# Attention walk of a decoder layer: written out without loops, with rotated queries and later tokens' inputs turned by DMA instead of by TensorE

## What is computed

```
q = rmsnorm(x @ w_qa, q_norm_w) @ w_qb                  # 16 heads of 128 + 64
q_nope, q_rope = (q[..., :DN], q[..., DN:])
kv = x @ w_kva
kv_c, k_rope = (kv[..., :KV_LORA], kv[..., KV_LORA:])
kv = rmsnorm(kv_c, kv_norm_w) @ w_kvb
...
q_rope = q_rope * cos + rotate_half(q_rope) * sin
k_rope = k_rope * cos + rotate_half(k_rope) * sin
scores = einsum('blhd,bmhd->bhlm', q, k) * scale        # causal mask
attn = softmax(scores)
out = einsum('bhlm,bmhd->blhd', attn, v).reshape(B, L, H * DV) @ w_o
```

## Time and profile before

| | |
|---|---|
| median of 3 runs | 1381.97 us (1381.57 to 1382.5) |
| profiled execution | 1380.98 us, its span 1379.2 us |
| PE busy | 1052.4 us, 76% |
| DVE busy | 1100.2 us, 80% |
| ACT busy | 539.6 us, 39% |
| POOL busy | 237.3 us, 17% |
| DMA, queue that SP issues to | 85.12 MB, 25.2% of 16 engines |
| granted TensorE clock, mean | 0.911 |
| DMA transposes | 256, median landing 2.8 us |

### The profile page before, as it was taken

One profiled execution on the slowest core, in us unless ns is written; L12 is line 12 of the kernel. 1 busy time (PEld: TensorE's weight loads), 2 busy tenths in 40 slices (PEclk: granted clock), 3 DMA queues, 4 the chain that ended last, 5 costly groups with the idle time before them and its releaser, 6 DMA issues.

```text
span 1379.2 us, 27210 instructions
## 1 busy us (share of the span) xinstructions
PE 1052.4 (76%) x7460; PEld 634.8 (46%) x7460; DVE 1100.2 (80%) x2984; ACT 539.6 (39%) x1225; POOL 237.3 (17%) x475
## 2 busy tenths in 40 slices
PE   1635587898988989989989999999652643447998
PEld 0423354555555555555555555555241322224554
DVE  5679587888888887987988888888169788886886
ACT  1549434443333434334333434344023330534443
POOL 1000012121121112112112112111003323122111
PEclk9659899999999999999999999999875766778999
DMA  9100022332322242222342232344560110000001
GB/s 361 47 1 0 1 58 56 62 61 53 58 51 55 57 116 53 57 51 48 61 116 48 56 60 55 60 118 75 163 214 9 52 31 0 0 0 8 30 38 46
DMA packets 199345, 85.73 MB, mean 62 GB/s; under 512 B 173560, under 2 KB 184824, under 8 KB 198784
## 3 DMA queue, kind: packets, MB, share of 16 engines
q1 hardware_dynamic: 199296, 85.12, 25.2%
HBM read 35.80 MB, written 7.34 MB: 31 GB/s over the span
## 4 chain that ended last, share of the span: by engine, by line
issue 35%; PE 27%; DVE 22%; POOL 8%; ACT 5%; DVEq 1%; DMA 1%; ACTq 1%; POOLq 0%; SPq 0%
PE bank L1778 5%; PE bank L1662 4%; DVE arena L1427 3%; PE bank L1728 3%; DVE arena L1444 2%; DVE arena L1451 2%; POOL arena L431 2%; PE bank L1763 2%; PE bank L1746 1%; PE bank L1750 1%; PE bank L1747 1%; POOL arena L1035 1%; PE bank L1749 1%; PE bank L1748 1%; DVE scal L1545 1%
## 5 line engine op out<-in xcount | busy, mean ns | idle before, releaser
L1173 ACT ACTIVATE arena<-bank,arena,scal 128x128 f32<-128x128 f32 (+3 forms) x256 | 157.8, 616 | 370.2 <-POOL arena L1031 370.2
L1778 PE MATMUL bank<-arena 128*128 (+1 forms) x768 | 180.7, 380 | 21.8 <-DVE arena L1457 10.8
L1451 DVE SCALAR_TENSOR_TENSOR arena<-arena 128x128 f16<-128x128 f32 (+3 forms) x256 | 169.3, 661 | 9.1
L1427 DVE TENSOR_REDUCE arena<-bank 128x1 f32<-128x128 f32 (+3 forms) x256 | 124.3, 486 | 52.9 <-PE bank L1751 51.1
L1031 POOL TENSOR_TENSOR arena<-arena,scal 128x1 f32<-128x1 f32 x256 | 48.5, 190 | 574.5 <-DVE arena L1427 574.5
L1728 PE MATMUL bank<-arena 128*128 (+1 forms) x576 | 136.5, 383 | 0.5 <-DVE arena L1483 0.5
L1763 PE MATMUL bank<-arena 128*128 128x512 f16 (+3 forms) x768 | 117.0, 303 | 19.3 <-DMA arena<-arena 10.7
L1778 PEld LDWEIGHTS bank<-arena 128*128 (+1 forms) x768 | 72.5, 97 | 102.0 <-issue 40.2
L1444 DVE TENSOR_SCALAR arena<-arena 128x128 f16<-128x128 f32 (+3 forms) x256 | 109.7, 429 | 5.6 <-DVE arena L1436 0.8
L1763 PEld LDWEIGHTS bank<-arena 128*128 (+1 forms) x768 | 69.2, 98 | 62.9 <-issue 26.0
L1746 PE MATMUL bank<-arena 128*128 (+4 forms) x256 | 77.7, 304 | 10.1 <-ACT arena L1173 3.6
(11 more groups left out here) (213 smaller groups left out, 2114.7 us busy)
## 6 DMA issues: line engine op xcount, KB each, us to landing
arena<-in_L_attn_w_qb SPq DMA_DIRECT2D x1, 4608.0 KB, 23.7
arena<-in_x SPq DMA_DIRECT2D x4, 1024.0 KB, 5.8
arena<-in_L_attn_w_o SPq DMA_DIRECT2D x1, 4096.0 KB, 34.0
arena<-arena SPq DMA_TRANSPOSE x256, 2.8
arena<-in_fside_BxS2xS SPq DMA_DIRECT2D x4, 1024.0 KB, 5.7
arena<-in_L_ffn_w SPq DMA_DIRECT2D x8, 512.0 KB, 7.6
out<-arena SPq DMA_DIRECT2D x16, 256.0 KB, 2.0
arena<-in_x SPq DMA_DIRECT2D x12, 256.0 KB, 3.0
```

Source lines behind the costliest of these rows:

```text
L1173: act.activation(pf(k), banks[S_BANKS[g % 3]][:, 0:n], ACT.Exp, bias=NB[:, k:k + 1], scale=sc_exp, accum_out=SUM[:, k:k + 1]).then_inc(s_e ...
L1427: dve.tensor_reduce(NEGM[:, (g & 3):(g & 3) + 1], banks[S_BANKS[g % 3]][:, 0:n], AX.X, ALU.max, negate=True).then_inc(s_max, 1)
L1451: dve.scalar_tensor_tensor(out=ph_part(k, 1), in0=pf(k).rearrange("p (t c) -> p t c", c=P), scalar=R4[:, k:k + 1], in1=ph_part(k, 0), op0= ...
L1778: last = pe.matmul(banks[Y_BANK][:, :], ot(gp, a, k, (q & 3) * P, P), wo(b, gp * GH + k), start=(k == 0 and n == 0), stop=(k == GH - 1 and ...
```

## The change

The loops over pairs go: all 32 pairs are written out with constants on every engine. The rotated queries of every pair are put side by side in one tile (RHL, 12 blocks of 128 columns: eight of high halves, four of low ones, ordered by head first and then by token tile), and SP turns them with one DMA transpose straight into QR. PE's `rope_t_hi` and `rope_t_lo` and DVE's two copies go. In the even pairs that prepare a tile, the rows (8 blocks), the rotary keys (3 blocks) and the latents (8 blocks) are turned by DMA too; PE's 19 transposes, ACT's copy and DVE's two copies go. The preparation is moved: `prep_mm` on PE from stage 2 to 3, the sums of squares, keys' rotation and the power on GpSimd from stage 3 to 4, the scaling from 4 to 5 and the split from 5 to 6. The rotary matmuls of the next pair wait for the rotation, no longer for the copy out. The first four tiles are prepared as before.

```diff
-        RH = take(TB * 2 * 2 * DR, fp16)
+        RHL = take(3 * L, fp16)
...
-        RL = take(TB * 2 * DR, fp16)
...
-        def walk(eng, pair):
-
-
-            def prep_of(d):
-                n = d + TB
-                return n, (n >> 2) & 1, n & 3
-
-            for d in range(3):
-                for j in range(2):
-                    pair(2 * d + j, j, first=(d + j == 0), prep=prep_of(d))
-            with eng.Fori(3, 12) as d:
-                prep = prep_of(d)
-                for j in range(2):
-                    pair(d * 2 + j, j, prep=prep)
-            with eng.Fori(12, 15) as d:
-                for j in range(2):
-                    pair(d * 2 + j, j)
-            for j in range(2):
-                pair(30 + j, j, last=(j == 1))
+        def walk(pair):
+
+            for i in range(NPAIR):
+                n = i // 2 + TB
+                pair(i, i & 1, first=(i == 0), last=(i == NPAIR - 1),
+                     prep=(n, (n >> 2) & 1, n & 3) if n < NT else None)
...
+            def turn_queries(i):
+
+                sp.wait_ge(r_split, i + 1)
+                if i >= 2:
+                    sp.wait_ge(s_mm, 8 * i - 8)
+                par = i & 1
+                sp.dma_start_transpose(QR[:, par * 1536:(par + 1) * 1536].rearrange("p (t q) -> p t q", t=12),
+                                       RHL).then_inc(r_in, 16)
+
+            def turn_x(n):
+
+                sp.wait_ge(xn_lo, n + 1)
+                sp.wait_ge(kv_mm, n)
+                sp.dma_start_transpose(XNT.rearrange("p (a q) -> p a q", a=8), XH).then_inc(xn_in, 16)
+
+            def turn_keys(n, par, tile):
+
+                sp.wait_ge(kr_made, n + 1)
+                sp.dma_start_transpose(part_kr(par, tile), KN).then_inc(kr_in, 16)
+
+            def turn_latents(n, par, tile):
+
+                sp.wait_ge(ch_lo, n + 1)
+                sp.dma_start_transpose(part_ct(par, tile), CH).then_inc(ct_in, 16)
+
             load_xt(TB)
+            turn_queries(0)
             for i in range(NPAIR):
                 for g in range(8):
                     turn_probs(i, g)
+                    n = i // 2 + TB
+                    if i % 2 == 0 and n < NT:
+                        if g == 0:
+                            turn_x(n)
+                        if g == 5:
+                            turn_keys(n, (n >> 2) & 1, n & 3)
+                        if g == 6:
+                            turn_latents(n, (n >> 2) & 1, n & 3)
+                    if g == 4 and i + 1 < NPAIR:
+                        turn_queries(i + 1)
...
-                v = RH.rearrange("p (a k d) -> p a k d", k=2, d=DR)
-                pool.tensor_tensor(RL.rearrange("p (a d) -> p a d", d=DR),
-                                   RT1.rearrange("p (a d) -> p a d", d=DR), v[:, :, 0, :], ALU.subtract)\
-                    .then_inc(r_split, 1)
+                low = RHL[:, 2 * L:3 * L].rearrange("p (t h d) -> p h t d", h=2, d=DR)
+                whole = RT1.rearrange("p (h t d) -> p h t d", h=2, d=DR)
+                high = RHL[:, 0:2 * L].rearrange("p (h t k d) -> p h t k d", h=2, t=TB, k=2)
+                pool.tensor_tensor(low, whole, high[:, :, :, 0, :], ALU.subtract).then_inc(r_split, 1)
...
                             prep_rstd(prep[0])
-                        if g == 3:
+                        if g == 4:
...
-                if not (isinstance(n, int) and n == 0):
+                if 0 < n <= TB:
                     act.wait_ge(xn_t, n)
+                if n > TB:
+                    act.wait_ge(xn_in, 16 * (n - TB))
...
-                    act.wait_ge(r_tl, i)
-                v = RH.rearrange("p (a k d) -> p a k d", k=2, d=DR)
+                    act.wait_ge(r_in, 16 * i)
+                v = RHL[:, 0:2 * L].rearrange("p (a k d) -> p a k d", k=2, d=DR)
...
-                    if prep is not None and (j, g) == (0, 4):
+                    if prep is not None and (j, g) == (0, 5):
                         prep_scale(prep[0])
                     if prep is not None and j == 0:
                         if g == 0:
                             prep_hi(prep[0])
-                        if g == 1:
-                            prep_te(prep[0])
-                        if g == 3:
+                        if g == 4:
                             prep_squares(prep[0])
...
-                dve.tensor_tensor(RT1, q, c, ALU.mult)
-                q4 = q.rearrange("p (a k d) -> p a k d", k=2, d=DR // 2)
-                s4 = s.rearrange("p (a k d) -> p a k d", k=2, d=DR // 2)
-                t4 = RT2.rearrange("p (a k d) -> p a k d", k=2, d=DR // 2)
-                dve.tensor_tensor(t4[:, :, 0, :], q4[:, :, 1, :], s4[:, :, 0, :], ALU.mult)
-                dve.tensor_tensor(t4[:, :, 1, :], q4[:, :, 0, :], s4[:, :, 1, :], ALU.mult).then_inc(r_rot, 1)
-
-            def rope_out_hi(i, par):
-                dve.wait_ge(r_th, i + 1)
-                dve.tensor_copy(QR[:, par * 1536:par * 1536 + 1024], bank16[R_BANK]).then_inc(r_teh, 1)
-
-            def rope_out_lo(i, par):
-                dve.wait_ge(r_tl, i + 1)
-                dve.tensor_copy(QR[:, par * 1536 + 1024:(par + 1) * 1536],
-                                bank16[Q_BANK][:, 0:L]).then_inc(r_tel, 1)
+                by_tile, by_head = "p (t h d) -> p t h d", "p (h t d) -> p t h d"
+                dve.tensor_tensor(RT1.rearrange(by_head, h=2, d=DR), q.rearrange(by_tile, h=2, d=DR),
+                                  c.rearrange(by_tile, h=2, d=DR), ALU.mult)
+                by_tile, by_head = "p (t h k d) -> p t h k d", "p (h t k d) -> p t h k d"
+                q4, s4 = (a.rearrange(by_tile, h=2, k=2, d=DR // 2) for a in (q, s))
+                t4 = RT2.rearrange(by_head, h=2, k=2, d=DR // 2)
+                dve.tensor_tensor(t4[:, :, :, 0, :], q4[:, :, :, 1, :], s4[:, :, :, 0, :], ALU.mult)
+                dve.tensor_tensor(t4[:, :, :, 1, :], q4[:, :, :, 0, :], s4[:, :, :, 1, :], ALU.mult)\
+                    .then_inc(r_rot, 1)
...
-                        if g == 3:
+                        if g == 4:
                             prep_var(prep[0])
                             prep_rope(prep[0], prep[2])
                             prep_srq(prep[0])
                             prep_rope_sum(prep[0])
-                        if g == 5:
+                        if g == 6:
                             prep_split(prep[0])
...
-                    if prep is not None and j == 1 and g == 1:
-                        prep_out(*prep)
...
-                pe.wait_ge(xn_te, n + 1)
+                if n < TB:
+                    pe.wait_ge(xn_te, n + 1)
+                else:
+                    pe.wait_ge(xn_in, 16 * (n - TB) + 16)
+                    pe.wait_ge(cf_made, n)
...
-                    pe.wait_ge(r_teh, i)
+                    pe.wait_ge(r_rot, i)
...
-            def rope_t_hi(i):
-                pe.wait_ge(r_hi, i + 1)
-                for t in range(TB):
-                    for h in range(2):
-                        last = pe.transpose(bank16[R_BANK][:, h * L + t * P:h * L + (t + 1) * P],
-                                            RH[:, (t * 2 + h) * P:(t * 2 + h + 1) * P], ident16[:, :])
-                last.then_inc(r_th, 1)
-
-            def rope_t_lo(i):
-                pe.wait_ge(r_split, i + 1)
-                if not (isinstance(i, int) and i == 0):
-                    pe.wait_ge(qn_lo, 2 * i + 1)
-                if not (isinstance(i, int) and i == 0):
-                    pe.wait_ge(r_tel, i)
-                bank = bank16[Q_BANK]
-                for t in range(TB):
-                    last = pe.transpose(bank[:, t * P:(t + 1) * P], RL[:, t * P:(t + 1) * P], ident16[:, :])
-                last.then_inc(r_tl, 1)
...
-                    pe.wait_ge(r_teh, i + 1)
-                    pe.wait_ge(r_tel, i + 1)
-                    pe.wait_ge(kr_te, 4 * (i >> 3) + 4)
+                    pe.wait_ge(r_in, 16 * i + 16)
+                    if i < 8:
+                        pe.wait_ge(kr_te, TB)
+                    else:
+                        pe.wait_ge(kr_in, 64 * (i >> 3))
...
-                    if prep is not None and j == 1 and g == 0:
-                        prep_t2(prep[0], i)
                     if prep is not None and j == 0:
-                        if g == 2:
+                        if g == 3:
                             if started(i - 5):
                                 pe.wait_ge(y_added, i - 4)
                             prep_mm(prep[0])
                     if g == 1:
                         nope_mm(i, 1)
-                        if prep is not None and j == 0:
-                            prep_t(prep[0])
                     if g == 4 and not first:
                         values(i - 1, 1)
                     if not last:
                         if g == 3:
-                            rope_mm(i + 1, prep if j == 1 else None)
+                            rope_mm(i + 1)
                         if g == 5:
```

(4 more changed lines are left out.)

47 lines of the change are left out of this document (21 added, 26 removed).

## The result

The changed kernel takes 1423.98 us (median, 1419.84 to 1424.92) beside 1381.77 us for the kernel before: a ratio of 1.0301, 95% interval 1.0279 to 1.0323. The prediction said 1358 us and gave 0.08 to a slower kernel. One execution of all those reported here, in the experiments (1553 us where the others of that kernel took 1406 to 1414), was far slower than the rest and is left out. The profiled execution has a span of 1423.1 us and a mean granted clock of 0.870 (0.911 before).

A forecast was written before the change was run, and what follows sets the result against it. Chains across DVE, PE and ACT, not busy sums, bound the kernel. Gains of 20.7, 9.0, 1.0 and 2.7 us gave 33.4, less 9.0 for the clock, 24.4: 1356.6 us profiled, 1358 median; range 1335 to 1378.

The forecast's parts named there:

- From there to the low part of block 4 ... 8.3 us. Sum 24.1, and the chain of 5.3: 29.4 us: Even pair with preparation: fifth maximum to block 4's low part 8.3 us; sum 24.1 plus queries' chain 5.3 makes 29.4 us.
- The clock, a loss ... One of two fell, so I take six: 9.0 us.: PE's idling in twelve even pairs lowers the clock in six of them, 1.5 us each: 9.0 us lost.
- The rival of the prediction: Every gap in the twelve even pairs lowers the clock, twice the price: 1367 us; chance 0.2.
- PE idles some 3 us: Even pair with preparation: PE idles some 3 us before the projections, waiting for the token rows' DMA transpose.
- At L1457 0.65 us: DVE's subtraction in the looped walk, register operations behind its wait for ACT: writing out saves 0.65 us per pair.
- The chain of 5.3 us: End of each pair: SP's issue 1.2 us, queries' transpose landing 3.5, next pair's first scores to DVE 0.6: 5.3 us.
- 15.9, and the chain 5.3: 21.2 us: Odd pair: 16.5 us less about 0.6 for PE's removed transposes is 15.9; with the queries' chain 5.3, 21.2 us.
- For a pair without preparation ... 21.4: Pairs 24 to 29: 21.4 us each where they took 22.9, 9.0 us gained over six pairs.
- Pairs 0 to 5 ... 1.0 us: First six pairs, straight code already: 3 x (50.9 - 50.6) = 1.0 us gained.
- Landing in proportion, 4.5 us: Queries' 12-block transpose lands after 4.5 us, each pair waits 1.0 us longer: 1389 us; chance 0.08.
- given-back rival: Straight program stalls on its loading, or rotation's regrouped accesses exceed 0.69 us; time stays about 1381 us; chance 0.04.
- the copies come back in full: Transfers land sooner, PE's gap is short, DVE is the bound and its removed copies are regained: 1333 us; chance 0.22.

The follow-up runs named there:

- 4: Changed kernel with scaling and its related preparation steps one stage earlier and 20 filler matmuls in PE's wait for the turned rows: 1361.1 us.
- 2: Changed kernel with squares, power, keys' rotation, scaling and split each one stage earlier, projections left at stage 3: 1379.8 us.
- 3: Changed kernel with 20 matmuls, whose results are overwritten, ahead of PE's wait for the turned rows: 1393.7 us.
- 1: Kernel before with its walk written out for all 32 pairs and nothing else changed: 1358.1 us.
- 5: Kernel before with walk written out, plus one half of the new DMA turning: queries alone 1375.3 us; rows, keys and latents alone 1411.2 us.
- 7: Queries' transpose issued before the fifth probability block's, GpSimd's low part earlier: 1407.5 us in the changed kernel, 1335.2 us in that with rows turned by PE.

## Why the prediction was wrong, point by point

- **"From there to the low part of block 4 ... 8.3 us. Sum 24.1, and the chain of 5.3: 29.4 us"** is the step that failed. From fifth maximum to low part it took 8.5 us (627.83 to 636.30), right; but the tail behind it was taken to be the queries' chain of 5.3 us, and it takes 8.3 (table in 4). PE was not there: moving `prep_scale` behind stage 5 made `project` at stage 6 stand still 3.45 us, since both use one PSUM bank and PE's program has `pe.wait_ge(cf_made, prep[0] + 1)` ahead of it. I had costed the moved work on DVE alone and not asked which matmuls are queued for its result. Moving all five steps back one stage gives back 44 us (2), about half of it by this wait and half by DVE's work, which the sum had.
- **"The clock, a loss ... One of two fell, so I take six: 9.0 us."** In the timeline ten of the twelve bursts of projections take 4.6 to 5.9 us and only two 3.1, and the lower level cost 2.9 us an even pair, not 1.5, and 30 us in all by the medians (3). The rival of the prediction had all twelve but half the price. The two stretches of the earlier trace rows were too few to go by. The Trainium skill ("TensorE: Matmul & The Clock Gate", HAM oscillation) had warned that waits for a DMA between bursts of matmuls lower the clock each time; here the trace agrees in ten waits of twelve (0.91 over pairs 6 to 23, against 0.98 with the gap filled).
- These two are the largest part of the error, not all of it. By the lengths of pairs the profiled execution is 68 us over the 1356.6 forecast for it: even pairs 6 to 22 +45, odd ones +10, pairs 24 to 29 +4, pairs 0 to 5 +13, pairs 30 and 31 and all behind the walk +5, less the 9.0 that the sum had set aside for the clock. That the kernel with both mended takes 1361 (4), beside the 1358 predicted, is in part luck: it pays nothing for the clock and has DVE's 2.2 us of preparation ahead of the fifth maximum, both of which the 1358 had paid for; without the clock's term alone the forecast would have been 1349.
- **"PE idles some 3 us"** for the rows: 3.75. The wait itself was seen, its size nearly.
- **"At L1457 0.65 us"** for the register work: right at that place, 0.66 a pair. But written out, the walk alone is worth 23 us (1), nearly all of the 24.4 that the sum ascribed to the whole change; that the two are so near is chance.
- **The chain of 5.3 us**: 5.7. Mis-sized were the landing (3.8, not 3.5) and by 0.1 the time from one issue to the next (1.27, not 1.2). **"15.9, and the chain 5.3: 21.2 us"** for the odd pair: 16.6 and 5.7, 22.3 in all. **"For a pair without preparation ... 21.4"**: 22.1. That the copies only turn into waiting was right, but it was not asked what the written-out walk would do without the chain: 21.4. The queries' part is a loss by itself of 17 us (5), and the sum had no row for it.
- **"Pairs 0 to 5 ... 1.0 us"** gained: 11.8 lost. The sum took all three couples of pairs for 50.9 us, as pairs 4 and 5; together the six took 147.9, not 152.8. Even ones went from 28.4 to 31.1 us, 2.3 of it the preparation work behind the fifth maximum (8.5 us to the low part, not 6.2) and 0.7 ahead of that maximum, where PE waits for the rows; the tail there did not grow. The odd pairs 1 and 3 took 20.1 us, less than the chain allows, and went to 21.7 and 22.6.
- **"The start: 2.7 us"**: 2.5 between low part and first score.
- **Landing in proportion, 4.5 us**, did not happen. The **given-back rival** is refuted: the walk alone shows no stall on loading, and the rotation's first product still takes 0.69 us. So is **the copies come back in full**: DVE is no bound where it idles 8.06 us ahead of one maximum.
- Not settled: 4 us that the changed kernel loses behind the walk. From the last maximum on, the profiled executions of the kernels with queries or rows by DMA take 2 to 7 us more than that of before, the written-out walk 0.4 more; busy times there are within 4 us of each other. Its cause is open.

## What to carry to other kernels

When a stage is moved back, list every instruction that waits for its result, also those that only want the bank, before costing the work itself: here a matmul that only wanted the bank stood still 3.45 us in nine pairs of 18. A gap ahead of a burst of matmuls is priced with the lower clock behind it, and filling the gap takes away the clock's part and leaves the wait, and so tells the two apart; making the input a whole pair earlier mends both. And a removed copy pays only if the transfer in its place is not last on a chain: here, with the rows turned by PE, putting the queries' transpose first on SP and their low part earlier on GpSimd (7) turned a loss of 12 us against the walk alone into a gain of 23.
